# Transposed copies of X by crossbar DMA, with X, XT and M in two buffers, other PSUM banks and another order of the work

## The reference

```python
mixed = silu(causal_conv(hidden @ w_qkv, conv_w))          # q, k, v of each head
beta, g = sigmoid(hidden @ w_b), -exp(A_log) * softplus(hidden @ w_a + dt_bias)
def step(state, xs):
    q_t, k_t, v_t, g_t, b_t = xs
    state = state * exp(g_t)[..., None, None]
    kv = einsum('bhk,bhkv->bhv', k_t, state)
    delta = (v_t - kv) * b_t[..., None]
    state = state + einsum('bhk,bhv->bhkv', k_t, delta)
    return state, einsum('bhk,bhkv->bhv', q_t, state)
o = rmsnorm(scan(step) * silu(hidden @ w_z)) * norm_gamma
x = layernorm(x + o @ w_out)
x = layernorm(x + experts_top2_of_8(x) + shared_expert(x))
```

## Time and profile before

| | |
|---|---|
| median of 3 executions | 2313.9 us |
| the profiled execution: span from first to last instruction | 2315.6 us |
| TensorE matmuls busy | 2275.0 us (98%) |
| TensorE weight loads busy | 1784.7 us (77%) |
| VectorE busy | 1953.3 us (84%) |
| ScalarE busy | 1326.1 us (57%) |
| GpSimd busy | 1204.2 us (52%) |
| DMA queue of SyncE, share of 16 engines | 11.8% |
| mean granted TensorE clock | 0.992 |

### The profile page before, as it was taken

One profiled execution on the slowest core, in us unless ns is written; L12 is line 12 of the kernel. 1 busy time (PEld: TensorE's weight loads), 2 busy tenths in 40 slices (PEclk: granted clock), 3 DMA queues, 4 the chain that ended last, 5 costly groups with the idle time before them and its releaser, 6 DMA issues.

```text
span 2315.6 us, 53894 instructions
## 1 busy us (share of the span) xinstructions
PE 2275.0 (98%) x20046; PEld 1784.7 (77%) x20046; DVE 1953.3 (84%) x3427; ACT 1326.1 (57%) x4125; POOL 1204.2 (52%) x1199
## 2 busy tenths in 40 slices
PE   6899999999999999999999999999999999999998
PEld 3687888878888778888788887888877888776665
DVE  5788888888888888888888888888888888885665
ACT  4565666656666656666566665666666666653110
POOL 4456555555555556555655556565565655552100
PEclk8999999999999999999999999999999999999999
DMA  4011111111001110111110111101111010120000
GB/s 140 20 38 56 38 38 38 56 38 56 27 30 56 38 56 32 44 38 56 38 48 28 38 56 38 56 20 56 38 56 38 30 46 38 38 90 1 28 10 19
DMA packets 32115, 98.46 MB, mean 43 GB/s; under 512 B 4336, under 2 KB 9840, under 8 KB 31600
## 3 DMA queue, kind: packets, MB, share of 16 engines
q1 hardware_dynamic: 31856, 95.02, 11.8%
HBM read 92.39 MB, written 2.62 MB: 41 GB/s over the span
## 4 chain that ended last, share of the span: by engine, by line
PE 97%; DVE 2%; ACT 1%; issue 1%; DMA 0%; POOL 0%; POOLq 0%; DVEq 0%; SPq 0%; ACTq 0%
PE bank L974 19%; PE bank L1001 10%; PE bank L1120 10%; PE bank L1075 5%; PE bank L548 5%; PE bank L1102 5%; PE bank L1014 5%; PE bank L1101 4%; PE bank L1034 4%; PE bank L1085 4%; PE bank L1024 4%; PE bank L1063 4%; PE bank L984 3%; PE bank L992 3%; PE bank L1040 3%; PE bank L1110 3%
## 5 line engine op out<-in xcount | busy, mean ns | idle before, releaser
L1278 DVE SCALAR_TENSOR_TENSOR conv<-bank,cw_all,conv 128x511 f32<-128x511 f32 (+2 forms) x768 | 564.7, 742 | 45.2 <-ACT conv L1170 40.3
L974 PE MATMUL bank<-xT,w_kh 128*128 128x512 f32 x1024 | 531.0, 602 | 2.8 <-ACT kraw L1198 1.8
L1170 ACT ACTIVATE conv<-bank,cw_all 128x512 f32<-128x512 f32 x256 | 176.8, 691 | 245.4 <-PE bank L974 245.4
L1314 DVE TENSOR_TENSOR N<-bank,lev 128x512 f16<-128x512 f32 x384 | 258.9, 674 | 56.7 <-PE bank L1024 56.7
L1215 ACT ACTIVATE X<-bank 128x512 f16<-128x512 f32 x384 | 229.0, 596 | 100.6 <-PE bank L1034 100.6
L1120 PE MATMUL bank<-wo,ogT 128*128 128x256 f32 x1024 | 268.7, 385 | 0.0
L887 POOL TENSOR_TENSOR keys<-kraw,kfac 128x1024 f32<-128x1024 f32 x64 | 121.4, 1897 | 277.8 <-PE bank L1085 277.5
L1001 PE MATMUL bank<-w_kh,xT 128*128 128x256 f32 x1024 | 263.9, 391 | 0.1
L926 POOL TENSOR_TENSOR ms<-ms,epsq 128x8 f32<-128x8 f32 x64 | 12.8, 199 | 388.7 <-ACT og L1230 388.7
L1024 PEld LDWEIGHTS bank<-X,mhiT 128*128 128x128 f16 x3072 | 135.9, 98 | 101.0 <-issue 46.5
L1034 PEld LDWEIGHTS bank<-N,XT 128*128 128x128 f16 x3072 | 131.8, 98 | 106.3 <-DVE N L1314 52.8
(11 more groups left out here) (181 smaller groups left out, 5651.2 us busy)
## 6 DMA issues: line engine op xcount, KB each, us to landing
egb<-rows SPq DMA_DIRECT2D x64, 512.0 KB, 4.9
ecb<-rows SPq DMA_DIRECT2D x64, 512.0 KB, 4.0
w_kh<-w_heads SPq DMA_DIRECT2D x16, 768.0 KB, 6.0
wo_raw<-w_out SPq DMA_DIRECT2D x16, 256.0 KB, 6.2
xT<-x_cols SPq DMA_DIRECT2D x4, 512.0 KB, 5.9
xT<-gate_up SPq DMA_DIRECT2D x1, 2048.0 KB, 7.7
ecb<-x_rows SPq DMA_DIRECT2D x3, 512.0 KB, 3.7
out<-og SPq DMA_DIRECT2D x3, 512.0 KB, 2.9
```

Of the source, the lines that this page charges most:

```text
L974: mm = pe.matmul(PB[j % 2][:, :], w[:, k, g * P:(g + 1) * P], xT[:, k, b * SEQ:(b + 1) * SEQ], start=(k == 0), stop=(k == KT - 1))
L1170: act.activation(conv[:, g, :], PB[i % 2][:, :], ACT.Copy, scale=cw_all[:, head, g * TAPS + 3:g * TAPS + 4]).then_inc(s_tap, 1)
L1278: dve.scalar_tensor_tensor(conv[:, g, m:], PB[j % 2][:, 0:SEQ - m], cw_all[:, head, g * TAPS + 3 - m:g * TAPS + 4 - m], conv[:, g, m:], op ...
L1314: dve.tensor_tensor(blocks(N[:, i], i, 0), packed(IB[1 - i % 2], i), blocks(lev[:, 1 + i:2 + i, :], i, 0).broadcast_to(shape), ALU.mult).t ...
```

## The change

- `growt` (TensorE and ScalarE) and `turned` (VectorE) are gone. In their place SyncE issues one `dma_start_transpose` of the whole X (128 x 1024 float16, 256 KB, from SBUF to SBUF) after each of the six levels, called `flip`; `growx` of the next level, and `finish` after level 5, wait for its completion (semaphores `s_xf`).
- X, XT, mhiT and mloT have two buffers, by parity of the body. N, which only `growx` still reads, keeps the joined half alone (64 columns per cell), also in two buffers, so the six copies on GpSimd that first filled it (`fill_n`, L838) are gone.
- PSUM: `join`, `growx`, the first half of the Newton step and k k^T use bank IB[parity]; q k^T and the second half use a bank Z; `read` and `write` use the first half of one bank R and `solve` the second half.
- Semaphores: `join` 0 no longer waits for `p`; `newton` 1 waits for it; `finish` 1 waits for both halves of `res`; `solve` waits for both cells of `rhs` at once.
- All orders are new, and SyncE has one of its own: loads and flips in one row.

```diff
     "sync": [
+        ("ecs", 0, 1), ("flip", 5, 0), ("flip", 0, 1), ("flip", 1, 1), ("egs", 0, 3), ("flip", 2, 1), ("flip", 3, 1),
+        ("flip", 4, 1), ("weights", 0, 2),
...
-        P0, P1, I0, I1, R0, R1, O0, O1 = bank
+        P0, P1, I0, I1, R, Z, O0, O1 = bank
...
-        X = sb("X", [P, CELLS, P], F16)
-        XT = sb("XT", [P, CELLS, P], F16)
-        N = sb("N", [P, len(LEVELS), CELLS, P], F16)
+        X = sb("X", [P, 2, CELLS, P], F16)
+        XT = sb("XT", [P, 2, CELLS, P], F16)
+        N = sb("N", [P, 2, CELLS, P // 2], F16)
...
+                elif name == "flip":
+                    p = n % 2
+                    sp.wait_ge(s_x[p], level(n, i))
+                    sp.dma_start_transpose(XT[:, p], X[:, p].rearrange("p a n -> p (a n)")).then_inc(s_xf[p], 16)
...
                 elif name == "growx":
-                    pe.wait_ge(s_n, 6 * n + i + 1)
-                    if 0 < i <= TURNED:
-                        pe.wait_ge(s_xv, TURNED * n + i)
-                    if i > TURNED:
-                        pe.wait_ge(s_xt, MATMUL_LEVELS * n + i - TURNED)
+                    pe.wait_ge(s_n[p], level(n, i))
+                    if i > 0:
+                        pe.wait_ge(s_xf[p], 16 * level(n, i - 1))
                     for x in range(CELLS):
-                        mm = pe.matmul(IB[i % 2][:, x * 64:(x + 1) * 64], XT[:, x, :], blocks(N[:, i, x:x + 1, :], i, 0),
-                                       start=True, stop=True)
-                    mm.then_inc(s_xgp, 1)
-                elif name == "growt":
...
+                        mm = pe.matmul(IB[p][:, x * 64:(x + 1) * 64], XT[:, p, x, :], N[:, p, x, :], start=True, stop=True)
+                    mm.then_inc(s_xgp[p], 1)
...
                 elif name == "finish":
                     pe.wait_ge(s_res, n * 2 + i + 1)
-                    pe.wait_ge(s_xt, MATMUL_LEVELS * (n + 1))
+                    pe.wait_ge(s_xf[p], 16 * level(n, 5))
```

More of the change, by code:

```diff
@@ L32 @@
     "tensor": [
[L33 to L42, removed]
@@ L43 @@
-        ("proj", 6, 3), ("join", 3, 2), ("write", 2, 1), ("proj", 7, 3),
+        ("vtp", 0, 2), ("vtp", 1, 2), ("join", 0, 2), ("vtp", 2, 2), ("newton", 0, 1), ("newton", 1, 1),
+        ("growx", 0, 2), ("vtp", 3, 2), ("gate", 0, 2), ("gate", 1, 2), ("gate", 2, 2), ("finish", 0, 1),
+        ("join", 1, 2), ("finish", 1, 1), ("proj", 0, 3), ("proj", 1, 3), ("gate", 3, 2), ("solve", 0, 1),
+        ("growx", 1, 2), ("turn", 0, 0), ("products", 1, 2), ("turn", 1, 0), ("proj", 2, 3), ("write", 0, 1),
@@ new lines @@
+        ("join", 2, 2), ("ktp", 0, 3), ("ktp", 1, 3), ("proj", 3, 3), ("read", 1, 1), ("growx", 2, 2), ("turn", 2, 0),
+        ("project", 0, 0), ("solve", 1, 1), ("project", 1, 0), ("write", 1, 1), ("products", 0, 3), ("join", 3, 2),
+        ("ktp", 2, 3), ("read", 2, 1), ("proj", 4, 3), ("growx", 3, 2), ("ktp", 3, 3), ("proj", 5, 3), ("join", 4, 2),
+        ("turn", 3, 0), ("out", 0, 1), ("solve", 2, 1), ("proj", 6, 3), ("write", 2, 1), ("proj", 7, 3),
+        ("project", 2, 0), ("growx", 4, 2), ("read", 3, 1), ("project", 3, 0), ("out", 1, 1), ("join", 5, 2),
@@ L44 @@
+        ("solve", 3, 1), ("out", 2, 1), ("out", 3, 1), ("growx", 5, 2),
     ],
     "scalar": [
[L46 to L49, removed]
@@ L52 @@
+        ("vals", 0, 3), ("power", 0, 1),
     ],
     "vector": [
[L54 to L57, removed]
@@ L815, in _, with decay_rows, run @@
             sp.wait_ge(s_rowd, 32)
-            for n in range(BODIES):
-                for dst, i, s_load, s_free, m in ((egb, 0, s_eg, s_scan, 2), (ecb, 1, s_ec, s_qe, 1)):
-                    if n > 1:
[L819 to L823, removed]
-            moe_loads(sp)
+            def decay_rows(dst, i, n, loaded):
+                sp.dma_start(dst[:, n % 2], rows[i, CELLS * n:CELLS * (n + 1)].rearrange("x t -> (x t)")
+                             .unsqueeze(0).broadcast_to([P, CELLS * P])).then_inc(loaded[n % 2], 16)
+            def run(name, i, n):
+                if name == "egs":
+                    if n > 1:
+                        sp.wait_ge(s_scan, 2 * (n - 1))
+                    decay_rows(egb, 0, n, s_eg)
+                elif name == "ecs":
+                    if n > 1:
+                        sp.wait_ge(s_qe, n - 1)
+                    decay_rows(ecb, 1, n, s_ec)
+                elif name == "flip":
+                    p = n % 2
+                    sp.wait_ge(s_x[p], level(n, i))
+                    sp.dma_start_transpose(XT[:, p], X[:, p].rearrange("p a n -> p (a n)")).then_inc(s_xf[p], 16)
+                elif name == "weights":
+                    if n % B == 1 and n // B + 1 < KH:
+                        weights(n // B + 1)
+            for name, i, n in rounds(ORDER["sync"]):
+                run(name, i, n)
+                if (name, i, n) == ("flip", 0, BODIES - 1):
+                    moe_first(sp)
+                elif (name, i, n) == ("flip", 5, BODIES - 1):
+                    moe_weights(sp)
+            moe_rows(sp)
         @block.gpsimd
@@ L940, in _ @@
             pool.wait_ge(s_gates, 12)
-            fill_n()
             scale_wo(0)
@@ L1153, in _ @@
                 run(name, i, n)
-                if n == 0 and (name, i) == ("proj", 3):
+                if n == 0 and (name, i) == ("proj", 2):
                     decays_tensor(pe)
```

205 lines of the change are left out of this document (101 added, 104 removed).

## The result

The changed kernel takes 2250.7 us, the median of four runs (2244.48 to 2251.76); the kernel before takes 2314.02 us in four runs (2312.9 to 2317.51). The ratio is 0.9718, with a 95% interval of 0.9703 to 0.9734: 63 us less. The forecast was 2252 us, 62 us less. The profiled execution has a span of 2249.0 us where the one before has 2315.6, and 2254 was forecast for it. Each run's time lies 1.7 us above its own span.

A forecast was written before the change was run, and what follows sets the result against it. TensorE's own list of matmuls was taken to bound the kernel. A body -0.95 - 0.16 + 0.10 = -1.01 us, by 64 -64.6; fill -4, drain +3, weights +4: together -62 us, so 2252 us, range 2235 to 2290.

The forecast's parts named there:

- `growt`, -0.95 us a body: On TensorE, eight matmuls in each of four levels go, 0.24 us a level: 0.95 us less a body.
- Fewer switches, -0.16 us a body: On TensorE, 12 float16 groups a round instead of 14, at some 0.08 us each: 0.16 us less a body.
- Handoffs, +0.10 us a body: Tight order on other engines, such as `silu` 3 and the copy of X on ScalarE: 0.1 us more a body.
- Flips: DMA transposes between levels: latency taken as 3.0 us, every window with 0.7 us or more to spare.
- Queue, +4 us: SyncE's queue: flip 5 behind weight loads, a wait of 0 to 2 us in each of 15 rounds, 4 us in all.
- rival C: SyncE's queue costs more: flip 5 waits 3 us behind weights, flip 2 behind `egb`; 2282 to 2322 us, chance 0.06.
- Fill, -4 us: Ahead of the first Newton step: k k^T comes about 8 us earlier, the first chain takes longer; 4 us less.
- Drain, +3 us: Last round with a chain: `proj`, `ktp` and half of `products` are missing, three windows fall short; 3 us more.
- A: Flip too slow for its windows at `growx` 2, 5 and `finish`; about 2477 us at the upper bound, chance 0.12.
- B: VectorE or ScalarE comes late, TensorE waits about a microsecond a round: 2310 us, no change; chance 0.04.
- the harsh form of rival A: The eight 128 x 128 blocks of one flip follow one another, each with its own latency: about 7000 us, chance 0.01.

The follow-up runs named there:

- experiment 3: Changed kernel with the eight matmuls of `growx` issued twice in levels 2 to 5: 2303.7 us, ratio 0.9948 to the kernel before.
- Experiment 1: Changed kernel with the load of the weights moved from behind flip 4 to behind flip 0: 2239.51 us, ratio 0.9672 to the kernel before.
- experiments 4 to 6: Changed kernel with the old order tables, 2744.48 us; with a large spare transpose ahead of each flip, 2470.8 us; with a small one, 2387.89 us.
- experiment 6: Changed kernel with a spare transpose of one 128x128 block ahead of each flip: 2387.89 us, ratio 1.0313 to the kernel before.
- experiment 5: Changed kernel with a spare transpose of seven 128x128 blocks ahead of each flip: 2470.8 us, ratio 1.068 to the kernel before.

## Why the prediction was right

Direction, mechanism and size were right: 2252 forecast, 2250.7 measured. Its terms were less good than its sum. Part of the closeness is also a step that went wrong: the forecast went from the span of 2254 us down by 1.7 to the median, because the profiled execution before lay that far above the median of its runs. The profiled execution after is one of the middle runs, and its time lies 1.7 us above its span of 2249.0. By spans the forecast was 5 us too high, by medians 1.3.

**`growt`, -0.95 us a body: right.** Eight matmuls still have a slot of 0.24 us in the slots of `growx` after; with them put back (experiment 3) 53 of the 63 us are gone again.

**Fewer switches, -0.16 us a body: a third of what the order gave.** The count was right, 14 groups before and 12 after. The step that failed is the one price of 0.08 us for each. Before, nine of the 14 stand ahead of ordinary matmuls and five ahead of PE transposes; after, it is three and nine. At 0.08 and 0.03 us that is 0.87 us before and 0.51 after: 0.36 saved. The clean round shows 0.50 (1.43 less the 0.93 of `growt`). The remaining 0.14 us is spread over parts and was not pursued.

**Handoffs, +0.10 us a body: nothing.** The clean round has no wait for VectorE or ScalarE, and from 100 to 2000 us all waits of PE that are not for flips come to 1.5 us. The busy time taken off the two engines is 2.3 us a body on VectorE and 1.9 on ScalarE (145.4 and 119.1 us by 64), where the forecast had 2.4 for each by adding up rows. Whether this relief is what kept the waits away wasn't tested.

**Flips: right.** Latency 3.0 taken, 3.1 measured; in the clean round the six windows are within 0.2 us of what was worked out (6.93 us for level 0 to 1, then 4.90, 5.78, 5.75, 5.10 and 5.16 from `growx` 5 to `finish`); `growx` of level 2, the tightest, never became the usual wait. The Trainium skill (Advanced Engine Details and Errata, section X-Bar Transpose (TRN2)) says that transposing DMAs are as fast as regular ones. In latency it nearly is so: 3.1 us for 256 KB beside 2.1 and 2.6. In engine time it is not: see the last section.

**Queue, +4 us: 16 us.** "A wait of 0 to 2 us is possible in each of 15 rounds" gave the right place and the right range, and too low a value in it. 13 of those rounds wait, 1.88 us at most, 12.0 us in all; the rest of the 16 us is four waits of `finish` in other rounds and three of `growx`. Experiment 1 shows that 11 us came from where the loads stand. That is the first half of rival C, flip 5 behind the weights, at a quarter of the 45 us it was priced at.

**Fill, -4 us: +1.7.** The first `join` is at 46.61 us where it was at 56.22: the start came 9.6 us earlier, 8 were forecast. But from there to the first Newton step it takes 30.8 us (46.61 to 77.40) where 19.5 were needed before and 23 were forecast. Windows ahead of the first `join` and from there to the first Newton step, as in the earlier trace rows, of the kernel before and of the kernel after:

```profile
0.00:56.22 56.22, 38.22 (x119) 19.17 (x119) 29.62 (x39) 23.96 (x49) 22.75 (x27) 0.88 0.43 145
56.22:75.69 19.47, 13.33 (x152) 9.05 (x151) 14.73 (x20) 12.42 (x35) 7.17 (x8) 0.81 0.01 2
...
0.00:46.61 46.61, 26.00 (x82) 11.61 (x83) 27.42 (x35) 20.18 (x42) 14.09 (x21) 0.93 0.38 129
46.61:77.40 30.79, 23.43 (x171) 15.75 (x170) 18.51 (x26) 14.40 (x39) 13.43 (x14) 0.83 0.39 98
```

The step that failed is the cost of the chain: the forecast counted only the chain's own links, and PE takes its list in order. In that stretch PE has 23.4 us of matmuls, where it had 13.3 before, and its idle time is 7.4 us, where it was 6.1; the longest wait in it is that of `growx` 5 for its flip, 2.75 us at 74.51, and the next that of `ktp` for ScalarE, 2.12 us at 63.74. The new order mostly moved work of PE from ahead of the first `join` (38.2 us before, 26.0 now) to behind it, into the chain. So the earlier start was no gain.

**Drain, +3 us: +4.8.** The mechanism named, windows that are too short because the next body's parts are missing, shows at `finish`, which waits 2.09 us for its flip at 2020.52, and at `growx` 2 of that chain, 0.80 us at 1997.68, which falls within the 63 rounds. The longest wait there is not a flip's: `growx` waits 2.95 us for N at 2005.45, while VectorE works for the experts, as a `growx` did before for 3.28 us at 2078.22. Behind the last Newton step PE's idle time grew by 1.9 us and its busy time by 2.9; what the latter comes from was not pursued.

**The sum.** Measured: 63 rounds of 1.43 us less are -90.1; +15.3 for what the mean round after (30.79 us) is longer than its clean one, against 16.0 us of waits for flips; +1.7 because the first and the last round before were shorter than 31.98 us; fill +1.7; drain +4.8: -66.6 us, where -62 was forecast. The order and the absent handoffs were better by 0.42 us a body, 26 us; queue, fill and drain were worse by some 20 us. The closeness of the total owes something to that, and so it is in part luck.

**The rivals.** A did not happen, but experiments 4 to 6 show how near it was: it needed only the old order, or 1.1 us more on the queue. Its price was also too low. In experiment 6 flips 1 to 4 land 4.3 us after X is ready; at L = 4.3 the forecast's sum for A gives 1.2 us a body, and the loss is 2.1. What the sum lacked is that each wait costs 0.16 us beyond what is shown, that a late level delays the flip behind it, and that flips 0 and 5 land later than the others (after 5.4 and 4.9 us there). B did not show. Of C the part with the weights did, at 11 us.

## What to carry to other kernels

Taking matmuls off a full TensorE by a DMA transpose pays if every transposed copy has its 3 us plus the handoffs covered by other matmuls, so add up the slots between a producer and its consumer for each level before moving anything; without that order the same change loses nearly seven times what it gains with it. Keep large loads out of the stretch of the queue ahead of the transposes with the least slack: moving one line of the issue order here was worth another 11 us. When pieces of float16 and float32 work alternate as here, put the float16 ones ahead of PE transposes rather than ahead of ordinary float32 matmuls, and price switches by what follows.

## What the runs showed of the hardware

- A DMA transpose takes DMA engine time well above its bytes. The queue's share went from 11.8% of 2315.6 us to 38.8% of 2249.0: 599 us more for 384 flips, 1.56 us of all 16 engines for 256 KB, or 168 GB/s by the bytes read, where plain loads ran at 389. The number of packets grew by 405,504, which is 1056 a flip, of about 250 bytes (100.7 MB more by 405,504). By the sentence of the Trainium skill cited above it would have been no more than the plain load; the trace doesn't agree.
- A transpose holds SyncE's queue for 1.11 us (128x128) to 1.24 us (128x1024), where the loads beside it hold it for 0.43 to 0.58. Eight blocks in one flip land in 3.1 us and one block in 2.2, so the blocks go side by side, and the harsh form of rival A, eight latencies in series, is far off.
- The first float32 matmuls behind a float16 group cost 0.08 us more, but PE transposes only 0.03.
- A wait of PE costs about 0.16 us beyond the idle time shown, since the next part no longer overlaps the end of the one ahead. One long wait cost more in experiment 5: `finish` stood 2.01 us idle at 1174.34, and the `proj` behind it took 3.21 us where the same four matmuls take 1.96 in the clean round, the granted clock being 0.57 from 1174 to 1178, so at 1.2 GHz for most of it. Waits that long are rare in the kernel after, and its mean granted clock is 0.992.
